# Cross-attention and FFN block: sums kept in PSUM, a deeper software pipeline and new orders on every queue

## The reference

```python
def layernorm(x): return (x - mean(x)) * rsqrt(var(x) + 1e-5)     # over the last axis
# cross-attention, 16 heads of 32 columns, 128 keys from ctx
q = layernorm(x) @ Wq;  k = ctx @ Wk;  v = ctx @ Wv               # split into heads
q = layernorm(q) * gq + bq;  k = layernorm(k) * gk + bk           # over the 32 columns of a head
p = softmax(q @ k.T / sqrt(32))
x = x + (p @ v) @ Wo
# FFN: 64 hidden values, each with 16 units of its own
s = layernorm(x) @ Win + bin_                                     # 512 -> 64
h = relu(s[..., None] * W1 + b1)                                  # 16 units per value
g = sum(h * W2, over the units) + b2
x = x + g @ Wout + bout
```

## Time and profile before

| what | value |
|---|---|
| median of 3 runs | 531.59 us |
| the profiled execution's own time | 534.23 us |
| its span, first to last instruction | 532.1 us |
| TensorE busy | 452.4 us, 85% |
| VectorE busy | 405.1 us, 76% |
| ScalarE busy | 300.7 us, 57% |
| GpSimd busy | 218.4 us, 41% |
| mean granted TensorE clock | 0.951 of full speed |

### The profile page before, as it was taken

The page is one execution under the profiler, slowest core; times in us unless marked ns, Lnnn a source line. Parts: engine busy times, 40 slices in busy tenths (PEclk is TensorE's granted clock), DMA queues, the critical chain, the costliest instruction groups (busy, mean ns, idle before and its releaser), DMA issues.

```text
span 532.1 us, 7537 instructions
## 1 busy us (share of the span) xinstructions
PE 452.4 (85%) x2392; PEld 304.8 (57%) x2392; DVE 405.1 (76%) x742; ACT 300.7 (57%) x539; POOL 218.4 (41%) x191
## 2 busy tenths in 40 slices
PE   5959957999989997998989998999899967975843
PEld 3646633676657754774567565765567535633732
DVE  3787962798689959994799869987996698546365
ACT  3468445737853688337752876259733872485042
POOL 3247612362555146622465246506554514102330
PEclk9998978999989999898999998999999988998896
DMA  8522576158015830387017811582058107801202
GB/s 309 158 77 81 129 152 139 62 117 198 24 38 151 213 78 21 118 184 176 22 63 165 203 28 45 152 193 51 1 156 202 41 0 179 200 22 59 89 11 79
DMA packets 25206, 58.31 MB, mean 110 GB/s; under 512 B 5840, under 2 KB 6352, under 8 KB 22096
## 3 DMA queue, kind: packets, MB, share of 16 engines
q1 hardware_dynamic: 24912, 57.57, 41.6%
q10 hardware_dynamic: 256, 0.26, 0.2%
HBM read 22.17 MB, written 8.39 MB: 57 GB/s over the span
## 4 chain that ended last, share of the span: by engine, by line
PE 52%; DVE 18%; DMA 8%; SPq 8%; ACT 5%; issue 5%; POOL 3%; DVEq 0%; ACTq 0%; POOLq 0%
PE bank L1719 33%; DVE hid L801 6%; DMA q_stack<-qt_hi 5%; PE bank L1725 5%; PE bank L1806 3%; PE bank L1818 3%; PE bank L1784 3%; ACT hid L1329 3%; PE bank L1821 2%; SPq L304 2%; DVE mx L727 2%; DMA q_stack<-mxt 2%; POOL at_lo L478 2%; SPq L264 2%; DVE at_lo L806 2%
## 5 line engine op out<-in xcount | busy, mean ns | idle before, releaser
L1260 ACT ACTIVATE prob<-bank 128x512 f32<-128x512 f32 x128 | 71.2, 597 | 30.6 <-PE bank L1806 20.1
L727 DVE TENSOR_REDUCE mx<-bank 128x4 f32<-128x512 f32 x128 | 81.0, 681 | 2.9 <-PE bank L1784 2.8
L473 POOL TENSOR_TENSOR qt_lo<-u,qt_hi 128x512 fp32r<-128x512 f32 x32 | 43.2, 1351 | 89.0 <-DVE u L719 89.0
L1818 PE MATMUL bank<-prob,v_kv 128*32 128x512 f32 x256 | 65.1, 622 | 3.4 <-ACT prob L1260 3.4
L462 POOL TENSOR_TENSOR squares<-u 128x512 f32<-128x512 f32 x32 | 36.0, 1124 | 70.9 <-DVE ssq L709 53.4
L1821 PE MATMUL bank<-prob,den_sel 128*32 128x512 f32 x256 | 64.4, 623 | 0.0
L1806 PE MATMUL bank<-q_stack,k_stack 97*128 97x512 f32 x128 | 50.3, 449 | 16.3 <-DMA q_stack<-qt_hi 7.9
L478 POOL TENSOR_TENSOR at_lo<-att,at_hi 128x512 fp32r<-128x512 f32 x32 | 40.4, 1291 | 47.6 <-ACT at_hi L1305 47.4
L1719 PE MATMUL bank<-wo_hi,at_hi 128*128 128x512 f32 x128 | 54.4, 425 | 4.6 <-POOL at_lo L478 4.6
L801 DVE SCALAR_TENSOR_TENSOR hid<-hid,w_col 128x512 f32<-128x512 f32 x56 | 53.4, 954 | 5.5 <-ACT hid L1329 1.6
L1719 PE MATMUL bank<-wq_hi,zt_hi 128*128 128x512 f32 x128 | 54.3, 424 | 3.7 <-DVE zt_lo L703 3.6
(11 more groups left out here) (136 smaller groups left out, 983.3 us busy)
## 6 DMA issues: line engine op xcount, KB each, us to landing
q_stack<-qt_hi SPq DMA_DIRECT2D x64, 256.0 KB, 5.1
xin<-in_x_dram SPq DMA_DIRECT2D x32, 256.0 KB, 3.1
q_stack<-qt_lo SPq DMA_DIRECT2D x32, 256.0 KB, 5.0
x<-in_x_dram SPq DMA_DIRECT2D x32, 256.0 KB, 3.2
out_dram<-x SPq DMA_DIRECT2D x32, 256.0 KB, 2.0
att<-in_L_xattn_Wk_dram SPq DMA_DIRECT2D x1, 1024.0 KB, 6.4
x<-in_L_xattn_Wq_dram SPq DMA_DIRECT2D x4, 256.0 KB, 7.4
hid<-in_L_xattn_Wv_dram SPq DMA_DIRECT2D x1, 1024.0 KB, 10.3
```

Of the source, the lines that this page charges most:

```text
L473: pool.tensor_tensor(qt_lo[:, :, cols], u[:, j, :].rearrange("p (i n) -> p i n", i=HC), qt_hi[:, :, cols].bitcast(F32), ALU.subtract).then ...
L727: dve.tensor_reduce(mx[:, j, :].rearrange("p (g i) -> p i g", g=G)[:, 2 * half:2 * half + 2, 2 * r:2 * r + 2], maxs_banks[T][half][j][r][: ...
L1260: act.activation(prob[:, h % PR, :], score_bank[t][h][:, :], ACT.Exp, scale=SCALE).then_inc(exp_done, 1)
L1818: pe.matmul(at_bank[t][c][rows(n), :], v_kv[kv_of(t)][:, n * HD:(n + 1) * HD], prob[:, n % PR, :], start=True, stop=True)
```

## The change

- The sum over the units lives in the PSUM bank of `project_s` (`s_bank`) and not in `hid`; the units then go round all four slots of `hid`, and `g_high` and `g_low` read the bank.
- The Newton step of the reciprocal writes into the bank of the denominators; `rden_err` is gone, and `rden_high` and `rden_split` read the bank.
- `q_full` moves from VectorE to ScalarE; `q_low` now waits for both of ScalarE's writes.
- Block 7 has buffers of its own, borrowed from tiles that are no longer needed: `u` for `att`, `wq_hi` and `wq_lo` for `at_hi` and `at_lo`, `qt_hi` and `qt_lo` for the split z2, `xin` for `x1`.
- Wo is loaded one place later on SyncE, and `wo_high`, `wo_low` and the split of Win move from the first 40 us to the end of the prologue.
- `selectors` moves from the end of VectorE's prologue to its start. `stack_keys(1)` moves behind `stack_q(0, 3)`.
- All orders and bank tables are new. On TensorE an iteration begins in the middle of the attention of block t-1 and ends in the middle of that of block t; it projects q of block t+2 (before t+1). On the other engines `iteration(t)` carries the output stages of block t-3. In the last stretch `project_o(6)` to `project_y(6)` stand behind `values(7, 7)`.

```diff
-        rden_err = sb("rden_err", [P, TOK])
+        def att_of(t):
+            return u if last(t) else att
+        def at_hi_of(t):
+            return wq_hi if last(t) else at_hi
+        def z2t_hi_of(t):
+            return qt_hi if last(t) else at_hi
+        def x1_of(t):
+            return xin if last(t) else x1
...
-                dve.tensor_tensor(rden_err[:, :], den_bank[t][:, :], rden[:, :], ALU.mult).then_inc(rden_step, 1)
+                dve.tensor_tensor(den_bank[t][:, :], den_bank[t][:, :], rden[:, :], ALU.mult).then_inc(rden_step, 1)
...
-                dve.scalar_tensor_tensor(out=rden[:, :], in0=rden_err[:, :], scalar=2.0, in1=rden[:, :],
+                dve.scalar_tensor_tensor(out=den_bank[t][:, :], in0=den_bank[t][:, :], scalar=2.0, in1=rden[:, :],
...
-                    dve.tensor_scalar(hid_slot(0), hid_slot(0), w2_col[:, 0:1], b2_col[:, 0:1], ALU.mult,
+                    dve.tensor_scalar(s_bank[T][:, :], hid[:, 0, :], w2_col[:, 0:1], b2_col[:, 0:1], ALU.mult,
...
-                    dve.scalar_tensor_tensor(out=hid_slot(0), in0=hid_slot(hh), scalar=w2_col[:, hh:hh + 1],
-                                             in1=hid_slot(0), op0=ALU.mult, op1=ALU.add).then_inc(hsum_done, 1)
+                    dve.scalar_tensor_tensor(out=s_bank[T][:, :], in0=hid[:, hh % RR, :], scalar=w2_col[:, hh:hh + 1],
+                                             in1=s_bank[T][:, :], op0=ALU.mult, op1=ALU.add).then_inc(hsum_done, 1)
...
-                dve.tensor_tensor(g_lo, hid_slot(0), g_hi.bitcast(F32), ALU.subtract).then_inc(g_done, 1)
+                dve.tensor_tensor(at_lo_of(T)[:, 0, :], s_bank[T][:, :], at_hi_of(T)[:, 0, :].bitcast(F32),
+                                  ALU.subtract).then_inc(g_done, 1)
...
+            def q_full(T, j):
+                act.wait_ge(q_turned, T * TB + j + 1)
+                act.activation(u[:, j, :], qt_bank[T][j][:, :], ACT.Identity, bias=bq_col[:, 0:1],
+                               scale=gq_col[:, 0:1]).then_inc(qf_done, 1)
```

More of the change, by code:

```diff
@@ L1170, in epilogue @@
                 add_hidden(7, 2)
+                residual2(6, 1)
                 add_hidden(7, 3)
@@ L1289, in rden_high @@
                 act.wait_ge(rden_done, t + 1)
-                if not first(t):
+                if last(t):
+                    act.wait_ge(q_done, BLOCKS * TB)
+                elif not first(t):
                     act.wait_ge(s_mm_done, t)
@@ new lines, in iteration @@
+                q_high(t, 0)
+                q_full(t, 0)
+                if t >= 2:
+                    rden_high(t - 2)
+                if t >= 3:
+                    move_rstd(t - 3)
+                q_high(t, 1)
+                if t >= 3:
+                    hidden(t - 3, 0)
+                if t >= 3:
+                    hidden(t - 3, 1)
+                if t >= 3:
+                    hidden(t - 3, 2)
+                z1_high(t + 1, 2)
+                q_full(t, 1)
+                move_u(t + 1, 0)
@@ new lines, in iteration @@
+                pe.wait_ge(zt_lo_done, t * 4 + 11)
+                max_scores(t + 1, 0, 1)
+                pe.wait_ge(att_done, t * 4 - 3)
+                scores(t, 0)
+                project_q(t + 2, 2, 1)
+                pe.wait_ge(zt_lo_done, t * 4 + 12)
+                turn_q(t + 1, 3)
+                pe.wait_ge(u_done, t * 4 + 10)
+                spread(t - 1, 1)
+                pe.wait_ge(mx_done[0], t * 8 + 11)
+                project_q(t + 2, 3, 0)
+                pe.wait_ge(qf_done, t * 4 + 7)
@@ new lines, in epilogue @@
+                scores(6, 2)
+                pe.wait_ge(exp_done, 97)
+                spread(5, 0)
+                pe.wait_ge(z2t_lo_done, 20)
+                pe.wait_ge(att_done, 21)
+                max_scores(7, 1, 1)
+                pe.wait_ge(exp_done, 98)
+                pe.wait_ge(mxt_done, 7)
+                max_scores(7, 0, 0)
+                pe.wait_ge(exp_done, 99)
+                turn_q(7, 3)
+                pe.wait_ge(qf_done, 30)
+                spread(5, 1)
+                pe.wait_ge(mx_done[0], 57)
@@ new lines, in epilogue @@
+                scores(6, 3)
+                pe.wait_ge(mx_done[1], 59)
+                spread(5, 2)
+                pe.wait_ge(g_done, 5)
+                project_y(4, 0)
+                pe.wait_ge(qf_done, 31)
+                project_y(4, 1)
+                pe.wait_ge(att_done, 22)
+                project_y(4, 2)
+                pe.wait_ge(exp_done, 100)
+                pe.wait_ge(mx_done[1], 60)
+                values(6, 0)
+                pe.wait_ge(qf_done, 32)
+                scores(6, 4)
@@ new lines, in epilogue @@
+                pe.wait_ge(out_done, 17)
+                project_y(4, 3)
+                pe.wait_ge(att_done, 23)
+                scores(6, 5)
+                pe.wait_ge(out_done, 19)
+                spread(5, 3)
+                pe.wait_ge(mx_done[0], 58)
+                pe.wait_ge(exp_done, 101)
+                max_scores(7, 0, 1)
+                values(6, 1)
+                pe.wait_ge(out_done, 20)
+                scores(6, 6)
+                pe.wait_ge(att_done, 24)
+                scores(6, 7)
@@ new lines, in epilogue @@
+                pe.wait_ge(mx_done[0], 63)
+                values(6, 4)
+                values(6, 5)
+                pe.wait_ge(mx_done[1], 64)
+                scores(6, 12)
+                pe.wait_ge(x1_done, 22)
+                scores(6, 13)
+                turn_z2(5, 0)
+                project_o(5, 2, 1)
+                pe.wait_ge(mx_done[0], 64)
+                turn_max(7)
+                pe.wait_ge(exp_done, 110)
+                project_o(5, 3, 0)
+                pe.wait_ge(mxt_done, 8)
@@ new lines, in epilogue @@
+                scores(7, 3)
+                pe.wait_ge(rstd_moved, 6)
+                spread(6, 0)
+                pe.wait_ge(att_moved, 28)
+                scores(7, 4)
+                pe.wait_ge(exp_done, 116)
+                scores(7, 5)
+                pe.wait_ge(rden_both_done, 7)
+                values(7, 0)
+                values(7, 1)
+                spread(6, 1)
+                pe.wait_ge(exp_done, 117)
+                scores(7, 6)
+                scores(7, 7)
+                pe.wait_ge(exp_done, 118)
```

2149 lines of the change are left out of this document (1079 added, 1070 removed), and 3 rows, old and new, of the table maxs_rows.

## The result

The changed kernel takes 486.96 us (median of four runs, 485.51 to 488.48). The kernel before took 532.0 us beside it (526.32 to 532.73), a ratio of 0.9175 with a 95% interval of 0.9105 to 0.9245. The forecast was 496 us with a range of 480 to 532. The profiled execution of the kernel after took 485.51 us.

What follows compares the result with a forecast made beforehand. TensorE, busy 85% of 532.1 us, was taken to bound the kernel. Losses of 10 + 7 + 24 + 24 = 65 us plus 431 of work gave a span of 496 and a predicted median of 496 us, range 480 to 532.

Steps and rivals of the forecast that it cites:

- the prediction's own formula: Loss in each stage is TensorE's idle time plus (1 - granted clock) x busy time; 101 us in the kernel before.
- start: First stage, 0 to 60 us: loss of 13.9 us becomes 10.
- second stage: 60 to 110 us, up to the first project_o of block 0: loss of 14.3 us becomes 7.
- middle: Six blocks from project_o of block 0 to that of block 6: loss 40 us becomes 24, 4.0 a block.
- end: From the first project_o of block 6 on: loss of 33 us becomes 24.
- waits per block: TensorE waits 1 us for low g, 1.5 to 2 at project_o(t-2, 0, 0); ScalarE 0 to 1 for q copies.
- Sums in PSUM: Unit sum in a bank: adds 0.954 to 0.75 us, together 2.4 us less VectorE per block.
- Full q on ScalarE: 4 x 0.80 us per block leave VectorE (to 41.7), 4 x 0.78 reach ScalarE (to 37.1).
- The deeper order: Middle blocks: the 2.37 us DMA wait for q goes; loss per block 4.0 us in place of 6.7.
- Half only: Rival: new order keeps its 6.7 us per block; median 512, or 523 if the prologue keeps its loss; chance 0.27.
- slower rival: A ScalarE wait at q_high(t+1, 0) for the q copies replaces the DMA wait; 543 us or more, chance 0.08.
- VectorE to PSUM costs its upper bound: Rival: adds into the bank take 1.84 us, 8.7 us more VectorE per block; 535 us; chance 0.10 with no change.

Runs made afterwards that it cites:

- version 12: Kernel after with first unit sum on ScalarE for blocks 0 to 5, two add_bout(6) behind the Newton step, two project_y(6) ahead of project_s(7): 487.97 us.
- run 2: Kernel after with the unit sum alone back in SBUF: 501.25 us, +14.3.
- run 1: Kernel after with unit sum and reciprocal's Newton step back in SBUF and q_full back on VectorE, new order kept: 518.46 us, 0.9767 of the kernel before.
- run 6: Kernel after with every copy of q into q_stack made twice, the second set waiting for the first: 604.26 us, +117.

## Why the prediction was right, and where it was off

**The size.** By the prediction's own formula, with the steady blocks taken one by one, the losses are now: start 9.3 us (10 predicted), second stage 6.9 (7), middle 15.8 (24), end 3.9 + 15.7 = 19.6 (24). Together 51.6 against 65, and fed work 483.7 - 51.6 = 432.1 against 431. The mis-sized term is the middle's "4.0 us of loss per block". In the three steady blocks it measured 0.85, 0.84 and 1.02; the other 13 us lie in the last three, whose order is written out one by one. So the measured 15.8 us come near the 2.5 us a block of the range's low end, but only as a mean of blocks that lose 1 us and blocks that lose much more. Of my waits per block, none is there: not the 1 us for g, not the 1.5 to 2 us at `project_o(t-2, 0, 0)`, not ScalarE's 0 to 1 us; and with no stops the clock is 1.00.

The end came out 4.4 us better. The step that failed is that the last wait of 10.46 us "stays". The four `project_y(6)` stand in that stretch now, two of them between its two waits, and TensorE is idle 3.88 + 2.53 = 6.41 us in it:
```profile
470.38 0.79 PE L1857 MATMUL bank<-wout_hi,at_hi 128*128 128x512 f32 x1 [3.88 <-DVE x L860]
...
475.83 0.50 PE L1857 MATMUL bank<-wout_hi,wq_hi 128*128 128x512 f32 x1 [2.53 <-DVE wq_lo L854]
```
The 4 x 0.6 us for `residual2(6)` were too much as well. From `spread_rstd(7)` to the end of the low part of g the chain takes 11.52 us, where it took 10.91, so 0.6 us more. TensorE is busy for 19.3 of the 21.7 us between the first `project_o` of blocks 6 and 7, as the signs of being right asked.

**Sums in PSUM.** The add at 0.75 us was right (751 ns, tail gone), and so was the low part of g at 0.69 (680 ns). The first unit was not: 0.81 instead of 0.75. Seven undisturbed adds take 5.90 us in the bank (version 12) and took 5.88 in SBUF, as forecast. The relief itself is smaller than its term: in the new order the undo gives VectorE 1.65 us a block, not 2.4. And I had wrong what it is worth. I counted VectorE's relief as room behind TensorE and gave the gain to the order; run 2 shows 1.65 us of period for 1.65 us of VectorE. By the prediction's formula, block by block, the order alone (run 1) still loses 35.8 us in the middle, where the forecast for it was 24; the kernel before loses 38.7 by the same count. So the order by itself doesn't do what the forecast gave to it, and that the total came within 9 us is in part luck.

The rule of the Trainium skill that speaks against a source in PSUM ("VectorE: DVE Perf Modes", the rules for kernel authors and the errata table) costs nothing here for an operation of two tensors: in the median 754 ns in the bank and 751 in SBUF (run 2). The prediction's comparison for it was a wrong reading, since its 0.68 us from PSUM is the row maximum, which has one tensor. The first unit has one tensor too, and there a bank costs time:
```profile
L849 DVE TENSOR_SCALAR hid<-hid,w_col,b_col x8: 537/546/1499, 155.1 to 483.7; 128x512 f32<-128x512 f32 x8
```
```profile
L845 DVE TENSOR_SCALAR bank<-hid,w_col,b_col x8: 804/810/814, 154.1 to 467.2; 128x512 f32<-128x512 f32 x8
```
546 ns with the sum in SBUF (first fence), 810 into the bank. The Trainium skill ("VectorE: DVE Perf Modes", section "Why PSUM operands drop a tier") says that an operand in PSUM takes the faster mode from float32 operations of one tensor; the two lines agree. It costs 0.26 us a block, small against the tail of 1.5 to 1.8 us that an SBUF operation can have.

**Full q on ScalarE.** 4 x 0.78 us, as forecast, and ScalarE at 37.2 us a block (37.1). VectorE fell to 43.4, not 41.7: my start of 47.3 was a mean that took in the shorter last block. The first three blocks had 48.5.

**The deeper order.** The DMA wait is gone, as predicted. ScalarE has room for the copies, 5.8 us in the block read in run 6, where I had expected a wait of 0 to 1 us. The forecast allowed 8 to 10 us for issue and landing; there they take 5.6, from 189.66 to 195.24 us.

**The start.** Both terms held (9.3 and 6.9). The undo of Wo's place cost 4.1 us where the first stage was to gain 3.9, that of the keys 4.3 where TensorE had stood 3.3. The move of `selectors` was not tried alone.

**The rivals.** *Half only* is what happens without the relief: run 1 gives 518 us in its 512 to 523. So the mechanism exists, and what decides between it and the result is VectorE's load, by which I had called it less likely. The slower rival's mechanism exists too: with the copies doubled, ScalarE waits 58 us for them. *VectorE to PSUM costs its upper bound* is out, by 757 ns for the longest add.

## What to carry to other kernels

An engine at 84% can be the bound. Compare its busy time and its idle time over two variants: if the idle stays constant while the busy time moves, and the same waits make it up, its stream is a loop of the period. In the old order the idle did not stay, and the relief brought less. The worth of a move hangs on the order around it: `q_full` on ScalarE was worth 2 to 4 us in the old order and 18.8 in the new, the keys' place 2 and 4.3. What brings nothing in one order should be tried again in the next. Stop relieving when TensorE's busy time meets the period: here the next 0.8 us off VectorE gave 0.15 us a block, and the next operation moved to ScalarE made the block 0.6 us longer.

## What the hardware showed that was not expected

- VectorE operations on 4 columns took 0.94, 1.20 and 1.22 us beside GpSimd's `att_low` (the first) and `add_bout`, and the latter two 0.16 and 0.17 with GpSimd held back (run 12). In the kernel after the first ends at 441.22 us and the third at 443.70, GpSimd's operations at 441.19 and 443.67. The Trainium skill ("SBUF — State Buffer", section "SBUF: two separate sides") says that VectorE and GpSimd share one pair of ports, held for a whole instruction, against operations with two SBUF inputs or in the faster mode. The rows agree: in the kernel after no add into the bank goes over 757 ns, and 56 in SBUF (run 2) reach 1726.
- A short operation held by a neighbour costs most where it stands in a chain with nothing behind it: three operations, two of which need 0.16 us undisturbed, were 3.4 us ahead of `spread_rstd(6)`.
- TensorE's clock in the last two `project_y` stretches, columns as in the earlier trace rows. In version 12, after 8.81 us without work, the granted clock was 0.50, which is the lower level, 1.2 GHz:
```profile
478.13:480.80 2.67, 2.67 (x6) 2.06 (x7) 1.24 (x2) 0.00 (x0) 0.00 (x0) 0.50 0.26 98
```
In the kernel after it was 1.00 (2.4 GHz) for the first three matmuls behind a gap of 2.53 us, and 0.55 behind them:
```profile
475.83:476.63 0.80, 0.80 (x3) 0.67 (x4) 0.55 (x1) 0.00 (x0) 0.00 (x0) 1.00 0.87 328
476.63:480.40 3.77, 3.77 (x10) 2.56 (x8) 2.08 (x3) 0.00 (x0) 0.00 (x0) 0.55 0.56 209
```
The fall comes later than the gap before it. The last twelve matmuls took 5.17 us of TensorE in version 12 and 4.60 in the kernel after. That they pay for `project_y(6, 0)` and `(6, 1)`, moved out of the gaps ahead of them, is a reading of one execution each; it was not tested by itself.
